# Self-attention stage of a convolution and mixture-of-experts kernel: the inverse root on ScalarE with a Newton step on VectorE, and the residual and normalising passes on GpSimd

## The chip, the cores and the metric

The kernel runs on 1 core of one Trainium2 chip. The metric is the device time of one execution in microseconds (us).

## The reference, cut to what matters

The model has a convolution-attention hybrid layer, a self-attention and a mixture of experts, on 8 images of 32 x 32 tokens with 256 channels. The change is in the self-attention, one pass per image over 1024 tokens:

```python
t = _to_tokens(x)                       # x after the hybrid layer: x + concat(conv, attention projection)
n = (t - mean(t)) / sqrt(var(t) + 1e-5)                       # _ln_t
Q, K, V = n @ W_q, n @ W_k, n @ W_v                           # 256 -> 128
w = softmax(Q @ K.T / sqrt(128))
t = t + (w @ V) @ W_o + b_o + n                               # the attention adds its own input n
# the experts then get _ln_t(t), a second normalisation of the same form
```

## The kernel before, in words

`self_attention` works image by image. 1024 tokens are 8 tiles of 128 tokens (`TT`); `QT` = 4 tiles are a half. For one image the steps are: `proj` (the earlier attention's projection: `att`, divided by the softmax sums `rsb` in the step `norm`, times `wp`, on TensorE, evicted by ScalarE into `mixT`); `mix` (transposes of `mixT`, added to `xb` by VectorE); `var` (mean and variance, `spread`, L1304); the inverse root `rstd`; `apply` (VectorE makes `shift` = -mean x rstd, ScalarE writes the normalised tokens `u`); `ut` (`u` transposed on TensorE, ScalarE rounds it to `uT_hi`, VectorE keeps the remainder `uT_lo`); `q`, `k`, `v`, `vt` (projections, each again as high and low part); `scores` (TensorE, then the row maximum on VectorE at L1312, then the exponential on ScalarE at L1227); `probs` (transposes of the probabilities, copied by ScalarE); `half` and `values` (probabilities times V); `out` (times W_o, and VectorE's b_t at L1361 adds `xb`); `vvar` and `vapply` (second normalisation, `rstdt` and `v2`, L1340); `turn` (transposes of `v2`).

The order of all engines' queues is written out by hand. An image's period has 8 slots. Each begins with `scores` of one tile, and then come the steps of `BETWEEN[slot]`, as (step, index, d): d = 0 is the image itself, d = 1 the next, d = -1 the one before. Each engine runs through the same list and does its own part, in order. Image 0 has no image before it, image 7 none after it. `FRONT` is the list for image 0's preparation ahead of the first period. `a_ps`, `b_ps` and `c_ps` are single PSUM banks: `ut` 1 can write `a_ps` only when the step `ut` 0 has been read by ScalarE and VectorE. `u` is one buffer for half an image.

What the change touches, as it is before:

- The inverse root is a power on GpSimd, 128x4 elements (L1214 for `rstd`, L1217 for `rstdt`).
- `apply` on VectorE writes `grow` = rstd + 1 and `shift` (L1327, L1328). ScalarE writes `u`, and 8 `grow` steps spread over the slots turn `xb` in place into xb x (rstd + 1) + shift, that is x + n (L1251). The step `res` adds b_o on VectorE (L1332).
- `norm`, the product `att` x `rsb`, is on VectorE (L1336), in slots 0 and 1; `proj` 0 is in slot 1 and `proj` 1 in slot 2.
- ScalarE loads its function table once, ahead of the stage (L1289): `nc.scalar.preload_act_table_set("natural_log_exp_and_others")`.
- SP loads `att` and `rsb` of the image after next once `proj` has read them.

`newton` (L46) is a helper of four dependent VectorE instructions with a drain behind each (L48, L50, L52, L54). Before, only the convolutions call it, on 128x2.

Of the kernel before, what the change touches and what calls it, by code (L numbers as in the profile page):

```python
# [7 lines left out]
ALU = mybir.AluOpType  # L8
# [962 lines left out]
def self_attention(nc, x, attn_w, attn_b, w_q, w_k, w_v, w_o, b_o, mixT_d, att_d, rsum_d, t_d, vT_d, vsum_d):  # L971
# [3 lines left out]
    with ExitStack() as ctx:  # L975
# [38 lines left out]
        vart, rstdt = (sb(f"b_{n}", [P, 2, QT]) for n in ("vart", "rstdt"))  # L1014
# [14 lines left out]
        var_ready, rstd_ready, shift_ready, u_ready, grown_ready, res_ready = (  # L1029
            sem(f"b_{n}_s") for n in ("var", "rstd", "shift", "u", "grown", "res"))  # L1030
# [38 lines left out]
        FRONT = [("norm", 0), ("norm", 1), ("proj", 0), ("proj", 1), ("mix", 0), ("mix", 1), ("mix", 2), ("var", 0), ("mix", 3), ("apply", 0), ("var", 1),  # L1069
# [28 lines left out]
        with nc.Block() as block:  # L1098
# [105 lines left out]
            @block.gpsimd  # L1204
            def _(pool):
                nc.gpsimd.memset(power[:], -0.5)
# [12 lines left out]
                all_images(pool, run)  # L1219

            @block.scalar
            def _(act):
                def run(steps):
                    for what, k, n, s in steps:
# [715 lines left out]
```

## Time and profile before

| | before |
|---|---|
| median of 3 runs | 2388.21 us |
| lowest and highest run | 2386.5 and 2390.58 us |
| the profiled execution's own time | 2386.5 us |
| its span | 2384.8 us |
| mean granted TensorE clock in it | 0.94 |
| TensorE, VectorE, ScalarE, GpSimd busy | 91%, 56%, 52%, 10% |

The profile is that of one execution, the 2386.5 us run. A row of the timeline gives start, duration (of a run of neighbouring instructions, where xcount is over 1), engine, line, operation, output <- inputs and their shapes; in brackets the idle time of the engine before it and what ended it. PE is TensorE's matmul, PEld its weight load, DVE VectorE, ACT ScalarE, POOL GpSimd, SP SyncE. The granted clock is a share of 2.4 GHz. A drain or a semaphore wait is not a row of its own.

### The profile page before, as it was taken

How to read it: one execution, taken by the hardware profiler on the slowest of the kernel's cores; microseconds unless marked ns; L12 is line 12 of the kernel's file. 1: busy time of each engine (PE TensorE's matmuls, PEld its weight loads, DVE VectorE, ACT ScalarE, POOL GpSimd, SP SyncE). 2: the span in 40 equal slices, each digit the busy share in tenths (PEclk: the TensorE clock that was granted, in tenths of full speed). 3: DMA queues.
4: the chain of work that ended last, by engine and by line, in shares of the span. 5: the costliest groups of instructions: out<-in, count | busy, mean ns of one | idle time of the engine just before them, and what ended most of it. 6: DMA issues, size and time to landing. Idle time of an engine off the chain costs nothing. (4 is left out here: it accounts for less than half of the span.)

```text
span 2384.8 us, 29739 instructions
## 1 busy us (share of the span) xinstructions
PE 2163.8 (91%) x10534; PEld 1496.6 (63%) x10534; DVE 1336.7 (56%) x1974; ACT 1234.4 (52%) x2160; POOL 249.2 (10%) x259
## 2 busy tenths in 40 slices
PE   4999999947899999999999983799999983999997
PEld 3777888846555455454554531577777772888886
DVE  6222333225777777777777712466666642565665
ACT  1111222222377777777777772466666642565664
POOL 1000000010031211222112300000000000000000
PEclk7999999965699999999999996999999996999999
DMA  2322243386776667776677303333333115334532
GB/s 74 85 83 66 67 137 119 120 165 189 214 109 118 110 106 111 109 117 109 103 118 109 111 10 93 117 102 102 105 110 107 44 54 199 124 131 177 186 123 63
DMA packets 150444, 268.01 MB, mean 112 GB/s; under 512 B 31809, under 2 KB 94017, under 8 KB 146241
## 3 DMA queue, kind: packets, MB, share of 16 engines
q1 hardware_dynamic: 141344, 240.76, 41.9%
q0 software_dynamic: 7680, 25.17, 3.3%
q8 instruction: 65, 1.06, 0.2%
q10 hardware_dynamic: 1312, 0.67, 0.1%
q14 instruction: 43, 0.34, 0.0%
HBM read 156.62 MB, written 107.25 MB: 111 GB/s over the span
## 5 line engine op out<-in xcount | busy, mean ns | idle before, releaser
L647 DVE TENSOR_REDUCE a_nmax<-a_sm 128x1 f32<-128x1024 f32 x512 | 603.8, 1219 | 195.2 <-PE a_sm L667 195.2
L903 ACT ACTIVATE p_shared<-a_st 128x512 f32<-128x512 f32 x1024 | 556.8, 597 | 234.8 <-PE a_st L928 233.2
L943 PE MATMUL a_pv<-p_shared,a_va 128*32 128x512 f32 x2048 | 272.5, 604 | 0.9 <-ACT p_shared L903 0.9
L928 PE MATMUL a_st<-a_qf,a_kf 121*128 121x512 f32 x704 | 253.8, 438 | 10.1 <-ACT p_shared L903 8.0
L667 PE MATMUL a_sm<-a_kf,a_qf 120*128 120x512 f32 x704 | 217.8, 429 | 42.3 <-DMA a_kf<-kq_d 27.5
L928 PEld LDWEIGHTS a_st<-a_qf,a_kf 121*128 121x128 f32 x704 | 119.0, 188 | 208.6 <-ACT p_shared L903 198.0
L1813 PE MATMUL x_h_ps<-x_v_hi,x_w 128*128 128x512 f32 x512 | 180.4, 394 | 25.7 <-DVE x_v_lo L1754 25.7
L667 PEld LDWEIGHTS a_sm<-a_kf,a_qf 120*128 120x128 f32 x704 | 135.9, 203 | 79.4 <-issue 27.6
L1827 PE MATMUL x_y_ps<-x_h_hi,x_w 128*128 128x512 f32 x512 | 178.0, 389 | 0.0
L1764 DVE SCALAR_TENSOR_TENSOR x_h_lo<-x_hid,x_wts,x_h_hi 128x512 fp32r<-128x512 f32 x128 | 96.0, 750 | 137.3 <-ACT x_h_hi L1735 137.3
L1731 ACT ACTIVATE x_hid<-x_h_ps,x_b 128x512 f32<-128x512 f32 x128 | 88.4, 691 | 130.2 <-PE x_h_ps L1813 125.2
L1813 PEld LDWEIGHTS x_h_ps<-x_v_hi,x_w 128*128 128x128 f32 x512 | 96.8, 189 | 45.5 <-issue 25.7
L1398 PE MATMUL b_o_ps<-b_pT,b_v 128*128 128x256 f32 x512 | 121.3, 380 | 0.0
L507 PE MATMUL c_acc<-c_y_hi,c_w_hi 128*128 128x512 f32 x288 | 117.6, 408 | 0.0
L507 PE MATMUL c_acc<-c_y_hi,c_w_hl 128*128 128x512 f32 x288 | 117.3, 407 | 0.0
L1227 ACT ACTIVATE b_probs<-b_s_ps,b_nmax 128x1024 f32<-128x1024 f32 x64 | 71.2, 1113 | 88.8 <-DVE b_nmax L1312 88.8
L507 PE MATMUL c_acc<-c_y_lo,c_w_hi 128*128 128x512 f32 x288 | 117.2, 407 | 0.0
L507 PE MATMUL c_acc<-c_y_lo,c_w_hl 128*128 128x512 f32 x288 | 117.1, 407 | 0.0
L507 PE MATMUL c_acc<-c_y_hi,c_w_lo 128*128 128x512 f32 x288 | 117.1, 406 | 0.0
L928 PE MATMUL a_st<-p_q_all,a_kf 121*128 121x512 f32 x320 | 112.4, 432 | 0.3 <-ACT p_shared L903 0.3
L1827 PEld LDWEIGHTS x_y_ps<-x_h_hi,x_w 128*128 128x128 f32 x512 | 96.1, 188 | 20.0
L928 PEld LDWEIGHTS a_st<-p_q_all,a_kf 121*128 121x128 f32 x320 | 53.7, 187 | 86.7 <-ACT p_shared L903 82.9
(242 smaller groups left out, 3609.4 us busy)
## 6 DMA issues: line engine op xcount, KB each, us to landing
x_w<-w_d SPq DMA_DIRECT2D x32, 1024.0 KB, 8.5
rel_d<-p_shared SPq DMA_DIRECT2D x12, 2048.0 KB, 12.2
a_qf<-rel_d SPq DMA_DIRECT2D x22, 512.0 KB
a_qf<-rel_d SPq DMA_DIRECT2D x44, 256.0 KB
c_xtok<-in_x SPq DMA_DIRECT2D x8, 1024.0 KB, 5.8
va_d<-c_va SPq DMA_DIRECT2D x16, 512.0 KB, 4.8
rel_d<-a_hl SPq DMA_DIRECT2D x4, 2048.0 KB, 20.7
a_va<-va_d SPq DMA_DIRECT2D x32, 256.0 KB
```

The costliest lines, as they stand in the source:

```text
L507: m = nc.tensor.matmul(image_rows(acc[u][:]), wt[:, k, :] if tap is None else wt[:, k, tap, :], y[s][:, k, rows + dy:rows + dy + H // 2, d ...
L647: nc.vector.tensor_reduce(nmax[:, h, t:t + 1], sm[k % 2][:], axis=AX.X, op=ALU.max, negate=True).then_inc(sm_read, 1)
L667: m = nc.tensor.matmul(sm[k % 2][:, cols], qf[j][0:ROW_M, h, half, t * P:(t + 1) * P], kf[j][0:ROW_M, h, cols], start=True, stop=True)
L903: nc.scalar.activation(probs[:, t % 2, h, half * HALF:(half + 1) * HALF], st[half][:], ACT.Exp).then_inc(exp_done, 1)
L928: nc.tensor.matmul(st[half][:], kf[j][0:ROW_M + 1, h, t * P:(t + 1) * P], qf[j][0:ROW_M + 1, h, 2 * t // TT, half * HALF:(half + 1) * HALF ...
L943: m = nc.tensor.matmul(pv[32 * h:32 * h + 32, cols], va[j][:, t, h, :], probs[:, t % 2, h, cols], start=t == 0, stop=t == TT - 1, skip_gro ...
L1227: nc.scalar.activation(probs[k % 2][:], s_ps[:], ACT.Exp, bias=nmax[:, k:k + 1], accum_out=ssum[:, k:k + 1]).then_inc(exp_done, 1)
L1398: m = nc.tensor.matmul(o_ps[:], v_sb[s][:, t, :], pT[k % 2][:, t, :], start=t == 0, stop=t == TT - 1)
L1731: nc.scalar.activation(hid[k % GB][:], h_ps[k % 2][:], ACT.Gelu, bias=b1_sb[s][:, e, f:f + 1]).then_inc(hid_ready, 1)
L1764: nc.vector.scalar_tensor_tensor(h_lo[k % HB][:], hid[k % GB][:], wts[s][:, e:e + 1], bits(h_hi[k % HB][:]), ALU.mult, ALU.subtract).then_ ...
L1813: m = nc.tensor.matmul(h_ps[k % 2][:], w[s][:, e, c, part, tile(f)], v[s][:, c, half(j)], start=i == 0, stop=i == 3 * KC - 1)
L1827: m = nc.tensor.matmul(y_ps[j][c][:], w[s][:, e, 2 + f // 2, part, f % 2 * C + c * P:f % 2 * C + (c + 1) * P], h[k % HB][:], start=first a ...
```

## The change

The inverse root is ScalarE's Ln and then Exp with scale -0.5, with a drain between, and VectorE then runs `newton` on the result, once in `apply` and once in `vapply`, ahead of its former work there. `grow` and `res` are gone. GpSimd instead adds `u` to `xb` and then b_o, after `u` is written; ScalarE's next `apply` waits for that, as `u` is one buffer. `norm` is done by GpSimd in its part of `proj`, and `proj` 0 moves from slot 1 to slot 0.

```diff
         BETWEEN = [
-            [("out", 2, -1), ("probs", 7, -1), ("norm", 0, 1), ("vt", 1, 0), ("turn", 0, -1), ("grow", 0, 0), ("grow", 1, 0)],
-            [("probs", 0, 0), ("proj", 0, 1), ("half", 3, -1), ("turn", 1, -1), ("norm", 1, 1), ("mix", 0, 1), ("grow", 2, 0)],
-            [("mix", 1, 1), ("values", 3, -1), ("probs", 1, 0), ("out", 3, -1), ("vvar", 1, -1), ("proj", 1, 1), ("var", 0, 1),
-             ("grow", 3, 0), ("grow", 4, 0)],
+            [("out", 2, -1), ("probs", 7, -1), ("proj", 0, 1), ("vt", 1, 0), ("turn", 0, -1)],
+            [("probs", 0, 0), ("half", 3, -1), ("turn", 1, -1), ("mix", 0, 1)],
+            [("mix", 1, 1), ("values", 3, -1), ("probs", 1, 0), ("out", 3, -1), ("vvar", 1, -1), ("proj", 1, 1), ("var", 0, 1)],
             [("probs", 2, 0), ("half", 0, 0), ("mix", 2, 1), ("apply", 0, 1), ("values", 0, 0), ("mix", 3, 1)],
             [("vapply", 1, -1), ("ut", 0, 1), ("probs", 3, 0), ("ut", 1, 1),
              ("probs", 4, 0), ("turn", 2, -1), ("var", 1, 1), ("q", 0, 1), ("v", 0, 1)],
-            [("turn", 3, -1), ("k", 0, 1), ("half", 1, 0), ("vt", 0, 1), ("apply", 1, 1), ("grow", 5, 0), ("res", 0, 0)],
-            [("out", 0, 0), ("values", 1, 0), ("ut", 2, 1), ("probs", 5, 0), ("out", 1, 0), ("ut", 3, 1), ("grow", 6, 0), ("grow", 7, 0)],
-            [("q", 1, 1), ("probs", 6, 0), ("res", 1, 0), ("vvar", 0, 0), ("half", 2, 0), ("k", 1, 1), ("vapply", 0, 0), ("v", 1, 1),
-             ("values", 2, 0)]]
+            [("turn", 3, -1), ("k", 0, 1), ("half", 1, 0), ("vt", 0, 1), ("apply", 1, 1)],
+            [("out", 0, 0), ("values", 1, 0), ("ut", 2, 1), ("probs", 5, 0), ("out", 1, 0), ("ut", 3, 1)],
+            [("q", 1, 1), ("probs", 6, 0), ("vvar", 0, 0), ("half", 2, 0), ("k", 1, 1), ("vapply", 0, 0), ("v", 1, 1), ("values", 2, 0)]]
...
             @block.gpsimd
-                        if what == "var":
-                            pool.wait_ge(var_ready, n * 2 + k + 1)
-                            nc.gpsimd.tensor_tensor(rstd[:, k], var[:, k], power[:], ALU.pow).then_inc(rstd_ready, 1)
-                        if what == "vvar":
-                            pool.wait_ge(vart_ready, n * 2 + k + 1)
-                            nc.gpsimd.tensor_tensor(rstdt[:, k], vart[:, k], power[:], ALU.pow).then_inc(rstdt_ready, 1)
+                        if what == "proj":
+                            pool.wait_ge(att_loaded[k], n * (16 * (1 + GROUPS)) + 16 * (1 + GROUPS))
+                            nc.gpsimd.tensor_tensor(att[k][:], att[k][:], rsb[k][:], ALU.mult).then_inc(norm_ready, 1)
+                        if what == "apply":
+                            x1 = xb[s][:, k * QT:(k + 1) * QT, :]
+                            pool.wait_ge(u_ready, n * 2 + k + 1)
+                            nc.gpsimd.tensor_tensor(x1, x1, u[:], ALU.add)
+                            pool.drain()
+                            pool.wait_ge(w_loaded, 16 * 5)
+                            nc.gpsimd.tensor_tensor(x1, x1, bo_all, ALU.add).then_inc(res_ready, 1)
...
             @block.scalar
+                def rsqrt(out, in_):
+                    nc.scalar.activation(out, in_, ACT.Ln)
+                    act.drain()
+                    return nc.scalar.activation(out, out, ACT.Exp, scale=-0.5)
...
+                        elif what == "var":
+                            act.wait_ge(var_ready, n * 2 + k + 1)
+                            rsqrt(rstd[:, k], var[:, k]).then_inc(rstd_ready, 1)
+                        elif what == "vvar":
+                            act.wait_ge(vart_ready, n * 2 + k + 1)
+                            rsqrt(rstdt[:, k], vart[:, k]).then_inc(rstdt_ready, 1)
                         elif what == "apply":
                             act.wait_ge(shift_ready, n * 2 + k + 1)
+                            act.wait_ge(res_ready, n * 2 + k + 1)
...
-                        elif what == "grow":
...
             @block.vector
+                def scales(m, r, v, tm, sh, ready):
+                    newton(nc, dve, r, v, tm)
+                    nc.vector.scalar_tensor_tensor(sh, m[:, :, 0], -1.0, r, ALU.mult, ALU.mult).then_inc(ready, 1)
...
                         elif what == "apply":
                             dve.wait_ge(rstd_ready, n * 2 + k + 1)
-                            nc.vector.tensor_scalar(grow[s][:, k], rstd[:, k], 1.0, None, ALU.add)
-                            nc.vector.scalar_tensor_tensor(shift[s][:, k], mv[:, :, 0], -1.0, rstd[:, k], ALU.mult, ALU.mult).then_inc(shift_ready, 1)
-                        elif what == "res":
-                            dve.wait_ge(grown_ready, n * TT + (k + 1) * QT)
-                            x1 = xb[s][:, k * QT:(k + 1) * QT, :]
-                            nc.vector.tensor_tensor(x1, x1, bo_all, ALU.add).then_inc(res_ready, 1)
-                        elif what == "norm":
-                            dve.wait_ge(att_loaded[k], n * (16 * (1 + GROUPS)) + 16 * (1 + GROUPS))
-                            nc.vector.tensor_tensor(att[k][:], att[k][:], rsb[k][:], ALU.mult).then_inc(norm_ready, 1)
+                            scales(mv, rstd[:, k], var[:, k], tmp[:, k], shift[:, k], shift_ready)
                         elif what == "vapply":
                             dve.wait_ge(rstdt_ready, n * 2 + k + 1)
+                            newton(nc, dve, rstdt[:, k], vart[:, k], tmpt[:, k])
```

## Rows read from the trace of the kernel before

**Rows 1.** Page, part 1: span, and busy time of TensorE.
```profile
span 2384.8 us, 29739 instructions
PE 2163.8 (91%) x10534; PEld 1496.6 (63%) x10534; DVE 1336.7 (56%) x1974; ACT 1234.4 (52%) x2160; POOL 249.2 (10%) x259
```

**Rows 2.** Busy time by window, one inner image (number 2).
```profile
core 0: us, PE busy (x) PEld busy (x) DVE busy (x) ACT busy (x) POOL busy (x), PEclk, DMA share, GB/s
1622.70:1680.70 58.00, 55.51 (x295) 44.43 (x294) 36.67 (x85) 37.47 (x74) 4.03 (x4) 1.00 0.33 105
```

**Rows 3.** Waits of TensorE, 1510 to 1960: total us, times, longest.
```profile
PE b_a_ps L1421 <- DVE b_uT_lo L1349: 12.0, 7, 2.5
PE b_a_ps L1421 <- ACT b_u L1245: 4.1, 6, 0.7
```

**Rows 4.** Timeline, slots 3 and 4 of image 2.
```profile
1646.27 2.07 ACT L1245 ACTIVATE b_u<-b_xb,b_shift,b_rstd 128x256 f32<-128x256 f32 x4
...
1647.84 1.22 DVE L1312 TENSOR_REDUCE b_nmax<-b_s_ps 128x1 f32<-128x1024 f32 x1 [0.70 <-PE b_s_ps L1383]
...
1648.98 1.37 DVE L1340 TENSOR_SCALAR b_v<-b_t,b_mvt,b_rstdt 128x256 f32<-128x256 f32 x4
...
1650.82 0.69 DVE L1349 TENSOR_TENSOR b_uT_lo<-b_a_ps,b_uT_hi 128x512 fp32r<-128x512 f32 x1 [0.47 <-ACT b_uT_hi L1255]
...
1651.57 0.65 PE L1421 MATMUL b_a_ps<-b_ident,b_u 128*128 128x128 f32 x4 [1.59 <-DVE b_uT_lo L1349]
```

**Rows 5.** Groups by line, GpSimd and ScalarE: busy us, mean ns, idle before.
```profile
L874 POOL TENSOR_TENSOR p_bd_lo<-a_w_st,p_bd_hi 128x512 fp32r<-128x512 f32 x32 | 41.9, 1310 | 12.9 <-issue 12.9
L266 ACT ACTIVATE c_sd<-c_gvar 128x2 f32<-128x2 f32 x8 | 1.6, 203 | 80.3 <-DVE c_gvar L324 80.3
L1289 ACT ACT_TABLE_LOAD x1 | 1.3, 1283 | 11.1 <-issue 11.1
```

**Rows 6.** Timeline of the convolutions, first image's normalisation.
```profile
26.53 5.18 POOL L244 TENSOR_TENSOR c_w_lo<-p_shared,c_w_hi 128x1152 fp32r<-128x1152 f32 x2 [20.25 <-DVE c_w_hi L435]
26.60 2.56 DVE L48 TENSOR_TENSOR c_tmp<-c_rstd 128x2 f32<-128x2 f32 x1
...
29.23 2.49 DVE L50 TENSOR_TENSOR c_tmp<-c_tmp,c_gvar 128x2 f32<-128x2 f32 x1
31.81 0.17 DVE L52 TENSOR_SCALAR c_tmp<-c_tmp 128x2 f32<-128x2 f32 x1
32.05 0.16 DVE L54 TENSOR_TENSOR c_rstd<-c_rstd,c_tmp 128x2 f32<-128x2 f32 x1
```

**Rows 7.** Timeline of the experts, one power on GpSimd.
```profile
2044.24 1.22 DVE L1754 TENSOR_TENSOR x_v_lo<-x_vT,x_v_hi 128x1024 fp32r<-128x1024 f32 x1
2044.41 1.92 POOL L1710 TENSOR_TENSOR x_rstd<-x_var,x_power 128x4 f32<-128x4 f32 x1 [55.89 <-DVE x_var L1782]
```

**Rows 8.** Tile `b_rstd`, 1480 to 1960: ns least/median/most, first and last start.
```profile
L1214 POOL TENSOR_TENSOR b_rstd<-b_var,b_power x15: 1007/1008/1013, 1481.0 to 1887.2; 128x4 f32<-128x4 f32 x15
```

**Rows 9.** Busy time by window, behind one TensorE wait in image 7.
```profile
1935.00:1939.00 4.00, 3.98 (x17) 3.66 (x18) 0.00 (x0) 1.75 (x5) 0.00 (x0) 0.57 0.00 0
```

**Rows 10.** Timeline of TensorE, three rows behind waits.
```profile
1536.54 0.66 PE L1421 MATMUL b_a_ps<-b_ident,b_u 128*128 128x128 f32 x4 [2.46 <-DVE b_uT_lo L1349]
...
1935.02 1.73 PE L1389 MATMUL b_pT_ps<-b_ident,b_probs 128*128 128x128 f32 x8 [2.68 <-ACT b_pT L1231]
...
1969.59 1.11 PE L1454 MATMUL b_c_ps<-b_ident,b_v 128*128 128x128 f32 x4 [5.67 <-DVE b_v L1340]
```

**Rows 11.** Timeline of the front, `norm` 1 of image 0.
```profile
1465.88 1.22 DVE L1336 TENSOR_TENSOR b_att<-b_att,b_rsb 128x1024 f32<-128x1024 f32 x1 [4.56 <-DMA b_rsb<-rsum_d]
```

**Rows 12.** Timeline, slot 1 of image 0.
```profile
1516.42 1.11 ACT L1227 ACTIVATE b_probs<-b_s_ps,b_nmax 128x1024 f32<-128x1024 f32 x1 [1.54 <-DVE b_nmax L1312]
...
1519.39 0.63 PE L1414 MATMUL b_a_ps<-b_ident,b_mixT 128*128 128x128 f32 x4 [1.53 <-ACT b_mixT L1238]
```

**Rows 13.** Timeline, slot 6 of image 2.
```profile
1665.18 1.10 ACT L1227 ACTIVATE b_probs<-b_s_ps,b_nmax 128x1024 f32<-128x1024 f32 x1
...
1668.10 0.60 PE L1421 MATMUL b_a_ps<-b_ident,b_u 128*128 128x128 f32 x4
```

More of the change, by code:

```diff
@@ L994, in self_attention @@
         st6, mv = sb("b_st6", [P, QT, 6]), sb("b_mv", [P, QT, 2])
-        var, rstd = (sb(f"b_{n}", [P, 2, QT]) for n in ("var", "rstd"))
-        grow, shift = ([sb(f"b_{n}{s}", [P, 2, QT]) for s in range(2)] for n in ("grow", "shift"))
-        power = sb("b_power", [P, QT])
+        var, rstd, tmp, shift = (sb(f"b_{n}", [P, 2, QT]) for n in ("var", "rstd", "tmp", "shift"))
         u = sb("b_u", [P, QT, C])
@@ L1013, in self_attention @@
         st6t, mvt = sb("b_st6t", [P, QT, 6]), sb("b_mvt", [P, QT, 2])
-        vart, rstdt = (sb(f"b_{n}", [P, 2, QT]) for n in ("vart", "rstdt"))
+        vart, rstdt, tmpt = (sb(f"b_{n}", [P, 2, QT]) for n in ("vart", "rstdt", "tmpt"))
         v2 = sb("b_v2", [P, QT, C])
@@ L1028, in self_attention @@
         c_read = sem("b_c_read")
-        var_ready, rstd_ready, shift_ready, u_ready, grown_ready, res_ready = (
-            sem(f"b_{n}_s") for n in ("var", "rstd", "shift", "u", "grown", "res"))
+        var_ready, rstd_ready, shift_ready, u_ready, res_ready = (sem(f"b_{n}_s") for n in ("var", "rstd", "shift", "u", "res"))
         uhi_ready, bhi_ready = sem("b_uhi_s"), sem("b_bhi_s")
@@ L1062, in self_attention @@
              ("probs", 4, 0), ("turn", 2, -1), ("var", 1, 1), ("q", 0, 1), ("v", 0, 1)],
-            [("turn", 3, -1), ("k", 0, 1), ("half", 1, 0), ("vt", 0, 1), ("apply", 1, 1), ("grow", 5, 0), ("res", 0, 0)],
-            [("out", 0, 0), ("values", 1, 0), ("ut", 2, 1), ("probs", 5, 0), ("out", 1, 0), ("ut", 3, 1), ("grow", 6, 0), ("grow", 7, 0)],
-            [("q", 1, 1), ("probs", 6, 0), ("res", 1, 0), ("vvar", 0, 0), ("half", 2, 0), ("k", 1, 1), ("vapply", 0, 0), ("v", 1, 1),
-             ("values", 2, 0)]]
-        FRONT = [("norm", 0), ("norm", 1), ("proj", 0), ("proj", 1), ("mix", 0), ("mix", 1), ("mix", 2), ("var", 0), ("mix", 3), ("apply", 0), ("var", 1),
+            [("turn", 3, -1), ("k", 0, 1), ("half", 1, 0), ("vt", 0, 1), ("apply", 1, 1)],
+            [("out", 0, 0), ("values", 1, 0), ("ut", 2, 1), ("probs", 5, 0), ("out", 1, 0), ("ut", 3, 1)],
+            [("q", 1, 1), ("probs", 6, 0), ("vvar", 0, 0), ("half", 2, 0), ("k", 1, 1), ("vapply", 0, 0), ("v", 1, 1), ("values", 2, 0)]]
+        FRONT = [("proj", 0), ("proj", 1), ("mix", 0), ("mix", 1), ("mix", 2), ("var", 0), ("mix", 3), ("apply", 0), ("var", 1),
                  ("ut", 0), ("ut", 1), ("apply", 1), ("sums", 0), ("q", 0), ("k", 0), ("v", 0), ("vt", 0), ("ut", 2), ("ut", 3), ("q", 1), ("k", 1), ("v", 1)]
@@ L1205, in _ @@
             def _(pool):
-                nc.gpsimd.memset(power[:], -0.5)
                 nc.gpsimd.memset(wp[:], 0.0).then_inc(consts, 1)
@@ L1211, in run @@
                     for what, k, n, s in steps:
[L1212 to L1217 removed]
+                        if what == "proj":
[8 more added lines that the diff above has]
+                            nc.gpsimd.tensor_tensor(x1, x1, bo_all, ALU.add).then_inc(res_ready, 1)
+                bo_all = bo[:].rearrange("p (a c) -> p a c", a=1).to_broadcast([P, QT, C])
                 all_images(pool, run)
@@ L1245, in run @@
                                 last = nc.scalar.activation(u[:, i, :], xb[s][:, k * QT + i, :], ACT.Identity,
-                                                            bias=shift[s][:, k, i:i + 1], scale=rstd[:, k, i:i + 1])
+                                                            bias=shift[:, k, i:i + 1], scale=rstd[:, k, i:i + 1])
                             last.then_inc(u_ready, 1)
-                        elif what == "grow":
-                            j, i = k // QT, k % QT
-                            nc.scalar.activation(xb[s][:, k, :], xb[s][:, k, :], ACT.Identity, bias=shift[s][:, j, i:i + 1],
-                                                 scale=grow[s][:, j, i:i + 1]).then_inc(grown_ready, 1)
                         elif what == "ut":
@@ L1357, in run @@
                             if k % 2 == 0:
-                                dve.wait_ge(res_ready, n * 2 + k // 2 + 1)
+                                dve.wait_ge(res_ready, n * 2 + k // 2 + 2)
                                 dve.wait_ge(t_stored[k // 2], n * 16 + 16)
@@ L1363, in run @@
                             last.then_inc(c_read, 1)
+                dve.sem_inc(res_ready, 1)
                 dve.wait_ge(sums_loaded[0], 16)
```

1 line of the change is left out of this document (removed).

## The prediction

> **What bounds the kernel now.** I read the page's busy times first [rows 1]: TensorE is busy for 91% of the span, VectorE and ScalarE for little over half, GpSimd for a tenth. The change touches one stage only, self-attention, from about 1442 to 1974 us, so I then read that stage in windows, one from each image's first scores to the next one's [rows 2]. An inner image takes 58.0 us, in which TensorE is busy for 55.5, VectorE for 36.7, ScalarE for 37.5 and GpSimd for 4.0. TensorE sets the pace, and lighter queues on VectorE and ScalarE can return only what TensorE now waits for. The waits [rows 3] say how much that is: 12.0 us for `b_uT_lo` in 7 waits and 4.1 us for `b_u` in 6. In each inner image both lie in slot 4 of `BETWEEN`. The timeline of one such place [rows 4] shows the chain: ScalarE writes `u`, VectorE takes the maximum of the scores, then does `vapply` (`b_v`), then the low part of `uT`, and TensorE, which needs its one PSUM bank back, stands until that low part is written (1.59 us). Whatever is put into VectorE's queue ahead of that low part goes straight into TensorE's wait. That is where the change must be priced.
>
> **The change part by part.** *Removed.* ScalarE loses 64 `grow` instructions, VectorE loses 16 `res` and 16 `norm` passes of 1.22 us (one of them in [rows 11]). Neither engine sets the end in the inner images, so these are worth nothing by themselves, except where named below.
>
> *GpSimd's new passes.* Per image it gets two `norm` products and four additions of 128x1024. The trace has no such pass; the nearest are 128x512 at 1.31 us [rows 5] and 128x1152 at 5.18/2 = 2.59 us [rows 6]. The slope is 1.28/640 = 2.0 ns an element, so 128x1024 is 1.31 + 512 x 0.002 = 2.33 us; bounds 1.31 and 2.59, and I take 2.33, for 1024 lies near the larger. The Trainium skill (GPSIMD Engine Reference, section "Performance versus the Vector engine") gives 4497 ns for an addition of 2048 elements, by an estimate half of it, 2.25 us, for ours; no run here shows that size, and the total would be 6 x 2 x 0.08 = 1 us lower by it. Six passes are 14 us of 58, so GpSimd's load fits easily.
>
> *Newton's step on VectorE, 32 times.* Its code also runs in the convolutions, beside long GpSimd passes, and that is the most telling place in the trace [rows 6]. The last two of its four small instructions take 0.17 and 0.16 us and start 0.24 us apart. The first two are TENSOR_TENSORs with both inputs in SBUF, on 128x2 elements, and last 2.56 and 2.49 us: the first ends at 29.16, when GpSimd's first pass ends (26.53 + 2.59 = 29.12), the second at 31.72, when its second ends. So a VectorE instruction with two SBUF inputs is held until the running two-input GpSimd pass is over. The reverse is seen among the experts [rows 7]: GpSimd's power, 1.01 us when left alone, takes 1.92 us beside a two-input VectorE pass. In the self-attention of before the same power takes 1007 to 1013 ns in all 15 cases of its window [rows 8], though much of VectorE's work with one input in PSUM runs then, so I hold only two-SBUF-input work to collide. Free of a collision a step costs 4 x 0.24 = 0.95 us.
>
> *Where they collide.* `vapply` of slot 4 now begins with Newton's step. In [rows 4] `u` of half 0 is complete at 1646.27 + 2.07 = 1648.34; GpSimd is idle and starts its first addition then, to 1650.7, and its second by about 1653.2. The step starts when the maximum ends, 1649.06, inside the first addition. Its first instruction is held to 1650.7; three more follow, and either the second or the fourth falls under the second addition and is held to about 1653.3. The step ends at 1653.5 (fourth held) to 1653.9 (second held), `vapply` takes 1.37 us more, and the low part of `uT` ends at 1653.55 + 1.4 + 0.7 = 1655.65 instead of 1651.51. TensorE's wait grows by 4.1 us, from 1.6 to 5.7. Bounds: 0.5 us (only the step, 0.95, less VectorE's slack of 0.47) and, with GpSimd passes of 2.59 us and both held, 4.9 us. It occurs where an image has both a predecessor (`vapply`) and a successor (`apply`): images 1 to 6. **6 x 4.1 = +24.6 us.**
>
> *The clock behind that wait.* After a wait of 2.68 us [rows 10] TensorE's granted clock was 0.57 on average over the next 4.0 us [rows 9], the lower level, 1.2 GHz, for most of it, and 4.0 x 0.43 = 1.7 us of work was lost; behind a wait of 5.67 us four transposes took 1.11 us, against 0.66 us behind one of 2.46 us [rows 10]. The new wait of 5.7 us is of the long kind, six times. Bounds: nothing and twice 1.7; I take 1.7, what the nearest row lost. **+10.2 us.**
>
> *Root on ScalarE instead of GpSimd.* Ln and Exp on 128x4 are bounded by nothing and 1.01 us (the power), nearest the Sqrt of 128x2 at 0.203 us [rows 5]; two and a handover are 0.47 us, less than the power. But they stand in ScalarE's queue, which waits there for the variance. Behind them stand `mixT` (slot 2), `q_hi` (slot 4) and `k_hi` (slot 7). They come about 1.7, 1.1 and 0.7 us later, against slack on TensorE of about 1.5 to 2, 0.6 beyond the delay, and 0.9. I cost this at nothing; if that slack were gone it would be up to 0.5 us in each of 7 images.
>
> *Slots 5 and 6.* Here GpSimd is idle when the step of `apply` runs, so it costs 0.95 us less 0.08 for the small addition that filled `grow`, 0.87. `u` starts that much later, but the following `grow` (0.6 us) is gone, so the exponential of 1665.18 starts 0.5 later, and so do `uT_hi`, `uT_lo` and the transposes that begin at 1668.10 [rows 13], after 0.2 us of TensorE's slack: 0.36 us in images 1 to 6 and 0.2 in image 0, **+2.4 us**.
>
> *`proj` 0 one slot earlier.* In inner images it covers a wait of 0.2 us in slot 0: **-1.2 us**. In image 0, slot 1, TensorE waited 1.53 us for `mixT` [rows 12]; with the product done a slot earlier its next scores can follow the exponential of 1516.42 by 1.26 us, at 1517.7 instead of 1519.8: **-2.1 us**. `norm` is out of the way, since GpSimd finishes the products of the next image some 2 to 3 us ahead of slot 0. SP's loads of `att` hang on `proj` and move with it; they are two slots early already.
>
> *Front and end.* `norm` 1 waits for its load until 1465.88 [rows 11] and heads the chain of the front; on GpSimd it takes 1.1 us more. The steps of `apply` 0 and 1 add 0.4 each: **+1.9 us**. At the end the last `vapply` gains 0.8 by the dropped `res` and loses about 0.5: **-0.3 us**.
>
> Sum: 24.6 + 10.2 + 2.4 - 1.2 - 2.1 + 1.9 - 0.3 = **+35.5 us**. The profiled execution took 2386.5 us, 1.7 outside its span and 1.7 below the median of the runs. 2386.5 + 35.5 = **2422 us**.
>
> **The rivals.** *A: no collision.* Newton's inputs are only 16 bytes a partition, and might slip in between. For it: the last two instructions in [rows 6] are quick; against it: the first two, of 8 bytes, were not. The terms beside it are +0.7, slot 4 costs 6 x 0.5 = 3.0: 2386.5 + 3.7 = 2390 us. *B: the relief wins (faster).* If VectorE is not held and ScalarE, rid of 38 us of `grow`, brings `u` and `uT_hi` forward, the waits of [rows 3] shrink; all 16.1 us would give 2370. It decides if the low part of `uT` in slot 4 ends before 1651.5. Against it: ScalarE starts `u` there behind a copy of probabilities, and no `grow` stands ahead of it in that slot. *C: one-SBUF-input work collides too.* Then the low parts, `t` and `mix` are held as well, about 5 us more in six images: 2452 us; [rows 8] speak against it. *D: table loads.* The stage loads its table once, by name (1.28 us, [rows 5]). If Ln and Exp each reloaded, 64 x 1.28 = 82 us would fall on ScalarE, about half on the path: 2463 us. The Trainium skill (ScalarE: Activation LUTs, section "Table sets: the hidden batching unit") has both functions in the named set, so one load, and prices a switch at about 2.7 us; were they separate, the loads would by it be 170 us and not 82. Whether Ln stays in that set no row shows, since before has none.
>
> **How the numbers follow.** Forecast 0.73, A 0.11, B 0.04, C 0.08, D 0.04. The forecast's own range: without the clock's loss and with 3.5 us a collision, 0.7 + 21 = +22 (2408); with 4.9 and twice the clock's loss, 0.7 + 29.4 + 20.4 = +50 (2437). The range reaches up over C and lets A, B and D go: 2404 to 2455. About 0.2% (4.8 us) can be told from no change. A lies near that mark, 0.08 within and 0.03 above: slower 0.73 + 0.08 + 0.04 + 0.03 = 0.88, same 0.08, faster 0.04.
>
> **What would show it.** In the timeline of slot 4, Newton's TENSOR_TENSORs lasting 1.5 to 2.5 us and ending with GpSimd's additions; TensorE's wait for `b_uT_lo` near 5.7 us six times, about 37 us in sum; the granted clock at its lower level after each; GpSimd's additions near 2.3 us; one table load in the stage. In slots 3, 5 and 7 the steps should take 0.9 us. Wrong it would be if the small instructions stay at 0.16 us beside GpSimd's passes (A), or if waits for `q_lo`, `k_lo` or `mixT` appear.

## The result, and the profile after

The changed kernel takes 2417.2 us (median of 4 runs, 2415.6 to 2418.75) and the kernel before 2387.4 us (4 runs, 2386.5 to 2390.6). The ratio is 1.0122, with a 95% interval from 1.011 to 1.0136: slower by 1.2%. The profiled execution took 2417.93 us, its span 2416.2, so 31.4 us more than the span in [rows 1]. Line numbers below are those of the kernel whose rows they are.

The head of the page of the changed kernel, against [rows 1]:

```profile
span 2416.2 us, 30025 instructions
PE 2175.0 (90%) x10534; PEld 1508.0 (62%) x10534; DVE 1342.2 (56%) x2054; ACT 1214.4 (50%) x2160; POOL 329.9 (14%) x274
```

TensorE does the same 10,534 matmuls and is busy 11.2 us longer for them, so part of the loss is slower matmuls and not idle time. VectorE is busy 5.5 us longer although 32 large passes left it.

TensorE's waits in the stage (total us, times, longest), against [rows 3]:

```profile
PE b_a_ps L1426 <- DVE b_uT_lo L1353: 35.7, 7, 5.6
PE b_a_ps L1426 <- ACT b_u L1259: 4.6, 7, 0.7
```

The wait for `b_uT_lo` has grown by 23.7 us. Its timeline in slot 4 of image 2 is the place of [rows 4]:

```profile
1652.68 1.22 DVE L1324 TENSOR_REDUCE b_nmax<-b_s_ps 128x1 f32<-128x1024 f32 x1 [0.70 <-PE b_s_ps L1388]
...
1653.27 2.35 POOL L1214 TENSOR_TENSOR b_xb<-b_xb,b_u 128x1024 f32<-128x1024 f32 x1 [30.72 <-ACT b_u L1259]
...
1653.83 1.81 DVE L48 TENSOR_TENSOR b_tmpt<-b_rstdt 128x4 f32<-128x4 f32 x1
...
1655.71 0.16 DVE L50 TENSOR_TENSOR b_tmpt<-b_tmpt,b_vart 128x4 f32<-128x4 f32 x1
1655.76 2.34 POOL L1217 TENSOR_TENSOR b_xb<-b_xb,b_bo 128x1024 f32<-128x1024 f32 x1
1655.95 2.18 DVE L52 TENSOR_SCALAR b_tmpt<-b_tmpt 128x4 f32<-128x4 f32 x1
1658.20 0.16 DVE L54 TENSOR_TENSOR b_rstdt<-b_rstdt,b_tmpt 128x4 f32<-128x4 f32 x1
1658.44 1.38 DVE L1344 TENSOR_SCALAR b_v<-b_t,b_mvt,b_rstdt 128x256 f32<-128x256 f32 x4
1659.74 0.68 DVE L1353 TENSOR_TENSOR b_uT_lo<-b_a_ps,b_uT_hi 128x512 fp32r<-128x512 f32 x1
1660.47 1.12 PE L1426 MATMUL b_a_ps<-b_ident,b_u 128*128 128x128 f32 x4 [5.64 <-DVE b_uT_lo L1353]
```

The first Newton instruction works on 128x4 elements and lasts 1.81 us; it ends at 1655.64, with GpSimd's first addition (1655.62). The second fits into the gap between the additions. The third, a TENSOR_SCALAR with one tensor read, lasts 2.18 us and ends at 1658.13, with the second addition (1658.10). What follows is late by as much, and TensorE stands for 5.64 us where it stood for 1.59. The four transposes behind it take 1.12 us instead of 0.65: the clock is down. There are six such waits of 5.64 to 5.65 us, one in each of images 1 to 6.

Images 1 and 2 from each first maximum of the scores to the next one's, by busy time (columns as in [rows 2]):

```profile
1563.93:1627.80 63.87, 57.37 (x293) 46.31 (x292) 38.25 (x95) 34.98 (x74) 14.13 (x6) 0.95 0.30 95
1627.80:1690.81 63.01, 56.52 (x295) 45.74 (x294) 38.25 (x95) 34.85 (x74) 14.14 (x6) 0.97 0.30 97
```

Measured so, the six images 1 to 6 take 379.2 us against 346.8 before, image 0 takes 51.7 against 53.95, the front from its first reciprocal to the first maximum 70.12 against 66.85, and the stages ahead of it ended 2.0 us sooner in this execution. With -0.4 for image 7 and the tail and +0.3 behind them, 32.4 - 2.25 + 3.3 - 2.0 - 0.4 + 0.3 = 31.35, the +31.4 of the spans.

### The profile page after: what moved, and what is told of

It reads as the page before. It is cut to its first block and busy times, and to the rows that moved or that the text cites. A ratio compares the mean times of both kernels' runs of the same rounds, so it can differ in the third digit from the quotient of the medians.

```text
span 2416.2 us, 30025 instructions
## 1 busy us (share of the span) xinstructions
PE 2175.0 (90%) x10534; PEld 1508.0 (62%) x10534; DVE 1342.2 (56%) x2054; ACT 1214.4 (50%) x2160; POOL 329.9 (14%) x274
## 5 line engine op out<-in xcount | busy, mean ns | idle before, releaser
L1324 DVE TENSOR_REDUCE b_nmax<-b_s_ps 128x1 f32<-128x1024 f32 x64 | 78.4, 1225 | 67.3 <-PE b_s_ps L1388 66.9
```

What stands on the lines that cost most here:

```text
L1324: nc.vector.tensor_reduce(nmax[:, k:k + 1], s_ps[:], axis=AX.X, op=ALU.max, negate=True).then_inc(max_ready, 1)
```

## The experiments

### The additions wait for `b_v`

GpSimd's additions of half 0 wait until slot 4's `vapply` is done, so that no Newton instruction of that slot meets them.

```diff
 pool.wait_ge(u_ready, n * 2 + k + 1)
+if k == 0 and not (isinstance(n, int) and n < 2):
+    pool.wait_ge(v_ready, n * 2 - 2)
```

> The changed kernel, but GpSimd starts its additions of half 0 only when the vapply of the image before has been written, so that Newton's step in slot 4 has the SBUF to itself; all engines do the same work. Theory 1 (GpSimd's passes hold VectorE's small instructions): Newton's instructions in slot 4 take 0.16 us each, TensorE's wait for b_uT_lo falls from 5.6 to about 2.1 us in six images, the clock stays high behind it, and the kernel comes to about 2388 us (-29). Rival (the cost is the longer queues on VectorE and ScalarE, not the collision): the work is the same, so 2417 us.

Measured: 2388.39 us (10 runs), ratio to the kernel before 0.9995 (0.9985 to 1.0004). One wait on GpSimd, which does the same work, gives the whole loss back. In its timeline of slot 4 Newton's instructions are short again and GpSimd starts behind `b_v`:

```profile
1648.92 0.15 DVE L48 TENSOR_TENSOR b_tmpt<-b_rstdt 128x4 f32<-128x4 f32 x1
...
1649.38 0.17 DVE L52 TENSOR_SCALAR b_tmpt<-b_tmpt 128x4 f32<-128x4 f32 x1
...
1649.87 1.38 DVE L1346 TENSOR_SCALAR b_v<-b_t,b_mvt,b_rstdt 128x256 f32<-128x256 f32 x4
...
1651.33 2.37 POOL L1216 TENSOR_TENSOR b_xb<-b_xb,b_u 128x1024 f32<-128x1024 f32 x1 [33.67 <-DVE b_v L1346]
...
1651.91 0.66 PE L1428 MATMUL b_a_ps<-b_ident,b_u 128*128 128x128 f32 x4 [1.98 <-DVE b_uT_lo L1355]
```

The wait is 1.98 us, 0.4 more than before: that is what Newton's step costs beside nothing. Images 1 to 6 take 348.0 us at a full granted clock, 5.2 us less each than in the changed kernel; 3.65 of it is the shorter wait and 1.55 is left for the clock. TensorE's busy time agrees: over the six images it is 9.9 us longer in the changed kernel for the same matmuls, 1.6 us an image.

### Newton's step out of slot 4

Is it the step itself, or the place? Two kernels take the step of slot 4 away. One moves it into slot 3:

```diff
-... ("apply", 0, 1), ("values", 0, 0), ("mix", 3, 1)],
+... ("apply", 0, 1), ("vnewton", 1, -1), ("values", 0, 0), ("mix", 3, 1)],
```

> The changed kernel, with the Newton step of vapply 1 taken out of slot 4 and put in slot 3 behind apply 0, where GpSimd is idle; same instructions, same total. Theory 1: the six waits fall to about 1.6 us and the kernel comes to about 2386 us. Rival (queue length): at most the step's own 0.95 us in six images is saved, so 2411 us or more.

The other drops it from both `vapply` steps, in slots 4 and 7:

```diff
 dve.wait_ge(rstdt_ready, n * 2 + k + 1)
-newton(nc, dve, rstdt[:, k], vart[:, k], tmpt[:, k])
 for i in range(QT):
```

> The changed kernel without Newton's step in vapply (the root of the second normalisation is left at ScalarE's Ln and Exp). What is then beside GpSimd's additions in slot 4 are the four TENSOR_SCALARs of 128x256 with their scalars from SBUF. If only instructions with two SBUF inputs are held, or this form is free: waits of 1.6 us, about 2385 us. If every TENSOR_SCALAR from SBUF to SBUF is held, as L52 was in the changed kernel (2.18 us): one or two of the four are held, the waits stay at 3.5 to 5.5 us, 2405 to 2417 us.

Measured: 2411.8 us (ratio 1.0089, 1.0072 to 1.0106) and 2412.5 us (1.0094, 1.0077 to 1.0111). Both win only 5 us, and where I had expected the first to be as fast as before, it was not. (The second lies in the range that I had given for the case that the TENSOR_SCALARs are held.) Timeline of slot 4 in the kernel without the step:

```profile
1653.23 2.36 POOL L1214 TENSOR_TENSOR b_xb<-b_xb,b_u 128x1024 f32<-128x1024 f32 x1 [30.70 <-ACT b_u L1259]
...
1653.79 5.08 DVE L1343 TENSOR_SCALAR b_v<-b_t,b_mvt,b_rstdt 128x256 f32<-128x256 f32 x4
...
1655.73 2.34 POOL L1217 TENSOR_TENSOR b_xb<-b_xb,b_bo 128x1024 f32<-128x1024 f32 x1
```

`b_v` itself, four TENSOR_SCALARs that take 1.38 us otherwise, is held over both additions, to 1658.87. The wait is 4.72 us six times in both kernels, 0.93 less than in the changed one, which is about the length of a free Newton step. So the step is the first to be caught, and not the whole cause: where it is gone, the TENSOR_SCALARs of `b_v` are caught in its place.

### One addition instead of two

GpSimd's second addition is left out.

```diff
-nc.gpsimd.tensor_tensor(x1, x1, u[:], ALU.add)
-pool.drain()
-pool.wait_ge(w_loaded, 16 * 5)
-nc.gpsimd.tensor_tensor(x1, x1, bo_all, ALU.add).then_inc(res_ready, 1)
+nc.gpsimd.tensor_tensor(x1, x1, u[:], ALU.add).then_inc(res_ready, 1)
```

> The changed kernel (2417.2 us) with GpSimd's second addition, that of b_o, left out: x1 is x + u alone (b_o is missing from the output). Theory 1 (a VectorE instruction that touches only SBUF and meets a GpSimd pass is held to the end of that pass, whatever its size): in slot 4 the first Newton instruction is held as now (about 1.8 us), the third is free at 0.17 instead of 2.18, TensorE's wait for b_uT_lo falls from 5.65 to about 3.5 us in images 1 to 6. That is 6 x 2.1 = -12.9 us, and 2 to 4 us more of the clock behind a shorter idle time: 2401 us. Theory 2 (what holds VectorE is that GpSimd is at work at all beside slot 4, so one hold grows as the other goes; or the b_v pass falls under what is left): waits stay above 5 us, 2415 to 2417 us.

Measured: 2403.3 us (ratio 1.0049, 1.0034 to 1.0064). Slot 4 of image 1, timeline:

```profile
1591.96 2.35 POOL L1214 TENSOR_TENSOR b_xb<-b_xb,b_u 128x1024 f32<-128x1024 f32 x1 [33.22 <-ACT b_u L1256]
...
1592.53 1.81 DVE L48 TENSOR_TENSOR b_tmpt<-b_rstdt 128x4 f32<-128x4 f32 x1
...
1594.65 0.17 DVE L52 TENSOR_SCALAR b_tmpt<-b_tmpt 128x4 f32<-128x4 f32 x1
...
1597.17 0.66 PE L1423 MATMUL b_a_ps<-b_ident,b_u 128*128 128x128 f32 x4 [3.64 <-DVE b_uT_lo L1350]
1597.67 1.81 PE L1391 MATMUL b_pT_ps<-b_ident,b_probs 128*128 128x128 f32 x8
```

The hold ends with the addition that is running, and the next instruction is held only if there is a next addition. The wait fell by 2.0 us, as theory 1 had it. The last row also shows that 3.64 us of standing still brought the clock down, though later: the first transposes are at full speed, the eight behind them take 1.81 us instead of 1.04. In busy time by window, images 3 and 4 of this kernel:

```profile
1688.56:1747.93 59.37, 54.77 (x292) 43.77 (x291) 36.25 (x95) 34.74 (x74) 9.41 (x4) 1.00 0.31 102
1747.93:1809.08 61.15, 56.68 (x294) 45.87 (x293) 36.25 (x94) 34.85 (x74) 9.40 (x4) 0.97 0.30 99
```

Image 3 kept the full clock and image 4 did not: 1.8 us between them. The other four are at 0.97 like image 4. The images are not quite alike, though: in the first experiment, all at the full clock, image 3 takes 57.71 us and image 4 58.27. Against the same image there, image 3 takes 1.7 us more and the other five 2.9 to 3.1, so the fallen clock costs 1.2 to 1.4 us.

### TensorE kept busy in the wait

Twelve matmuls 128x512 whose result nobody reads stand ahead of turn 1 of `u` in images 1 to 6, so that TensorE does not idle for so long and the collision stays as it is.

```diff
 elif what == "ut":
+    if k == 1 and not (isinstance(n, int) and n < 2):
+        pe.wait_ge(b_read, n * NB + b_at("q", 0) + 1)
+        for _ in range(12):
+            nc.tensor.matmul(b_ps[:], w_hi[:, 0, 0, :], w_hi[:].rearrange("p k t u -> p (k t u)")[:, 0:HALF],
+                             start=True, stop=True)
     pe.wait_ge(a_read, n * NA + a_at("ut", k) + 1)
```

> The changed kernel, with 12 matmuls without use (128x512 into a free PSUM bank, about 2.8 us) put into TensorE's wait of 5.6 us in images 1 to 6; the wait's end does not move. If the clock's fall behind the wait costs what the prediction said (1.7 us, six times): the granted clock stays at 1.00 there and the kernel comes to about 2407 us. If the slower clock is hidden: 2417 us. If 2.8 us of work are not enough to keep the clock: 2417 us with the clock still low.

Measured: 2412.3 us (ratio 1.0088, 1.0071 to 1.0104), 5 us less than the changed kernel, between the 2407 us of a clock kept everywhere and the 2417 us of one kept nowhere. Two of its images, by window:

```profile
1567.50:1629.25 61.75, 57.83 (x305) 46.18 (x304) 38.33 (x94) 34.73 (x74) 14.18 (x6) 1.00 0.30 99
...
1753.96:1817.10 63.14, 59.39 (x307) 47.94 (x306) 38.30 (x95) 34.83 (x74) 14.17 (x6) 0.97 0.29 96
```

The fill kept the clock up in four images of six. These four take 61.5 to 62.0 us, the other two 62.7 and 63.1, and those of the changed kernel 62.6 to 63.9. The four average 61.7 us against 63.2 for the six of the changed kernel, 1.5 us less. Against the same images of the first experiment the four take 3.7 to 3.8 us more and the other two 4.9 to 5.0. So a kept clock is worth 1.2 to 1.5 us an image.

### Which forms of instruction are held

A small program behind the kernel's end meets 13 forms of VectorE instruction, each once with GpSimd idle, once under an addition of two SBUF tiles and once under a multiplication of one tile by a constant.

```diff
+dve.sem_inc(go, 1)                                              # GpSimd starts its pass
+nc.vector.tensor_reduce(pad[:], acc[:], axis=AX.X, op=ALU.max)  # 0.7 us, reads PSUM
+dve.drain()
+test(form, out)
```

> The changed kernel with a small program behind its end: 13 forms of VectorE instruction, each met three times: with GpSimd idle (tile name ending in free), under a GpSimd addition of two SBUF tiles 128x1024 (ending in add), and under a GpSimd multiplication of one SBUF tile 128x1024 by a constant (ending in cpy). Each instruction starts about 0.7 us after the GpSimd pass, so that a hold to the end of the addition shows as about 1.6 us more. Theory 1 (held: what reads and writes SBUF alone, one or two inputs, except the statistics): tt_small, ts_small, stt_small, recip, ts_ptr, ts_imm, copy, tt_two about +1.6 us under the addition; tt_ps, stt_ps, copy_ps, stats, reduce within 0.1 us of free. Theory 2 (held: two SBUF inputs, and the tensor_scalar and copy forms, which run at twice the rate: 128x256 in 0.3 us rather than 0.6; everything at one element a cycle with one SBUF input is free): as theory 1 but recip and reduce, and perhaps ts_small, free; a form's free time tells which. Under the multiplication by a constant both theories leave open whether anything is held. The kernel's own part should show the times of the changed kernel; the total is longer by some 150 us.

Timeline of the first form. The test instruction ends with the addition (2424.00), and not with the multiplication (2427.00):

```profile
2421.39 0.16 DVE L1949 TENSOR_TENSOR m_tt_small_free<-m_src,m_oth 128x4 f32<-128x4 f32 x1
2421.66 2.34 POOL L1972 TENSOR_TENSOR m_o<-m_z,m_y 128x1024 f32<-128x1024 f32 x1 [0.55 <-DVEq L1991]
...
2422.45 1.57 DVE L1949 TENSOR_TENSOR m_tt_small_add<-m_src,m_oth 128x4 f32<-128x4 f32 x1
...
2424.21 2.79 POOL L1974 TENSOR_SCALAR m_o<-m_z 128x1024 f32<-128x1024 f32 x1 [0.21 <-DVEq L1987]
2424.98 0.29 DVE L1949 TENSOR_TENSOR m_tt_small_cpy<-m_src,m_oth 128x4 f32<-128x4 f32 x1
```

All 39, in ns, as the trace gives them:

| VectorE instruction | GpSimd idle | under the addition | under the multiplication |
| --- | --- | --- | --- |
| TENSOR_TENSOR, two SBUF, 128x4 | 164 | 1566 | 290 |
| SCALAR_TENSOR_TENSOR, two SBUF, 128x4 | 164 | 1583 | 285 |
| TENSOR_SCALAR, constants, 128x4 | 170 | 1597 | 283 |
| TENSOR_TENSOR, two SBUF, 128x256 | 425 | 1850 | 548 |
| TENSOR_SCALAR, scalars from SBUF, 128x256 | 414 | 1715 | 411 |
| TENSOR_SCALAR, constants, 128x256 | 295 | 1717 | 414 |
| COPY, SBUF, 128x256 | 295 | 1718 | 417 |
| RECIPROCAL, SBUF, 128x4 | 178 | 177 | 178 |
| BATCH_NORM_STATS2, SBUF, 128x256 | 428 | 427 | 428 |
| TENSOR_REDUCE, SBUF, 128x256 | 420 | 420 | 420 |
| TENSOR_TENSOR, PSUM and SBUF, 128x256 | 425 | 425 | 425 |
| SCALAR_TENSOR_TENSOR, PSUM and SBUF, 128x256 | 425 | 425 | 425 |
| COPY, PSUM, 128x256 | 424 | 424 | 425 |

Under the addition seven forms are held to its end, and six are not touched at all. Under the multiplication nothing is held, and six of those seven forms take about 0.12 us more. Theory 2 has the right list; theory 1, which had the statistics and the reduction free as well, falls with RECIPROCAL, which reads SBUF alone and is free. Theory 2's own test, that the free time tells which form is held, fails for one form: the TENSOR_SCALAR with scalars from SBUF. The Trainium skill (SBUF — State Buffer, section "Who interferes with whom") gives this list almost whole: VectorE and GpSimd share a pair of ports, which two SBUF inputs need, and which copies and TENSOR_SCALARs can take in a double-rate mode, while a reduction never does. The COPY and the TENSOR_SCALAR with constants agree (295 ns, against 424 ns for the COPY from PSUM). The one with scalars from SBUF (414 ns) shows no double rate and is held all the same. By that section whoever comes second is fully blocked; the addition agrees, the multiplication, which reads SBUF as well, does not: the measurement decides, +0.12 us and no block.

### `proj` 0 back in slot 1

From the kernel of the first experiment, one part of the change is taken back.

```diff
-[("out", 2, -1), ("probs", 7, -1), ("proj", 0, 1), ("vt", 1, 0), ("turn", 0, -1)],
-[("probs", 0, 0), ("half", 3, -1), ...
+[("out", 2, -1), ("probs", 7, -1), ("vt", 1, 0), ("turn", 0, -1)],
+[("probs", 0, 0), ("proj", 0, 1), ("half", 3, -1), ...
```

> The kernel of the first experiment (the changed kernel with GpSimd's additions behind b_v, 2388.4 us), with one part of the change taken back: projection 0 of the next image stands in slot 1 behind the first transposes again, as before the change, the division stays on GpSimd. Theory 1 (the prediction's terms of -1.2 us an inner image and -2.1 us in image 0 are right and come from this move): 2388.4 + 6 x 1.2 + 2.1 = 2397.7 us, with a wait or a stretch of lower clock ahead of slot 2 of each image. Theory 2 (the move is worth nothing, and the shorter image 0 comes from the growth's absence on ScalarE): 2388 us within 1.

What I expected here misread the prediction: its -1.2 us is the sum over the inner images, 0.2 us each, so that theory 1, by the prediction's own terms, is 2388.4 + 1.2 + 2.1 = 2391.7 us.

Measured: 2392.8 us, ratio 1.0009 (1.0 to 1.0018), against 0.9995 of the kernel that it differs from: the move is worth some 3 to 4.5 us, close to the 3.3 us of the prediction. In its trace image 0 takes 53.77 us against 51.71, and the wait of [rows 12] is back. Images 1 to 5 take 0.4 us more on average. Image 6 takes 1.5 us more, because TensorE's granted clock fell in it (0.97 over the image, 0.83 from 1892 to 1900 us) behind the same wait of 2.0 us for `b_uT_lo` that left the clock full in the other five images.

```profile
1523.50 0.63 PE L1421 MATMUL b_a_ps<-b_ident,b_mixT 128*128 128x128 f32 x4 [1.53 <-ACT b_mixT L1247]
```

### Image 0's divisions on VectorE

```diff
-if what == "proj":
+if what == "proj" and not (isinstance(n, int) and n == 0):     # GpSimd
...
+elif what == "proj" and isinstance(n, int) and n == 0:          # VectorE
+    dve.wait_ge(att_loaded[k], 16 * (1 + GROUPS))
+    nc.vector.tensor_tensor(att[k][:], att[k][:], rsb[k][:], ALU.mult).then_inc(norm_ready, 1)
```

> The kernel of the first experiment (2388.4 us) with the two divisions of image 0, in the front, on VectorE rather than on GpSimd. Theory 1 (the front's +3.2 us against the kernel before are the longer GpSimd passes ahead of projections 0 and 1, 2.34 us each against 1.2 to 1.3 on VectorE): front shorter by 2 to 3.2 us, 2385.7 us. Theory 2 (the front is longer for the additions of u on GpSimd, or for transfers): 2388 us, front as in the first experiment.

Measured: 2389.9 us, ratio 0.9994 (0.9985 to 1.0003), against 0.9995 of the kernel it starts from. In the profiled execution the front is 4.0 us shorter (66.2 us against 70.2). Most of that is TensorE's clock: projection 1 ran at the full clock (1.90 us instead of 3.67), and the transposes of `mixT` behind it are through in 5.4 us instead of 6.8. Projection 1 itself starts 0.7 us sooner. The ratios show nothing of it, and each is known to about 2 us either way. What the divisions cost in the front is left open between nothing and some 3 us.

### Towards a faster order

Three kernels try to get rid of the 2 us that are left. The first starts from the kernel of the last experiment and takes the first low part ahead of `b_v`:

```diff
-[("vapply", 1, -1), ("ut", 0, 1), ("probs", 3, 0), ("ut", 1, 1),
+[("ut", 0, 1), ("vapply", 1, -1), ("probs", 3, 0), ("ut", 1, 1),
```

> The kernel of the experiment with image 0's divisions on VectorE (GpSimd's additions behind b_v; 2389.9 us, ratio 0.9994), with one step moved: in slot 4 VectorE subtracts the low part of turn 0 of b_u before it writes b_v rather than behind it (GpSimd's additions wait for b_v as before and start 0.7 us later). In the profile of the first experiment ScalarE's high part was ready at 1650.73 and VectorE's low part began at 1651.17. Theory 1 (VectorE's b_v is what is late): the wait of 2.0 us falls by 0.45, 7 x 0.45 = -3 us, 2386.5 us. Theory 2 (ScalarE's high part, behind the exponential, is what is late, and b_v then delays the second low part, which began 1651.17 + 2.06): what is won ahead of the second turn is lost behind it, 2389 to 2391 us.

The second also puts scores 5 into the gap; the third does that to the kernel before:

```diff
+[("ut", 0, 1), ("vapply", 1, -1), ("probs", 3, 0)],
+[("ut", 1, 1), ("probs", 4, 0), ("turn", 2, -1), ("half", 1, 0), ("var", 1, 1), ("q", 0, 1), ("v", 0, 1),
+ ("turn", 3, -1), ("k", 0, 1), ("vt", 0, 1), ("apply", 1, 1)],
```

> As the previous kernel, and slot 4 is cut short: scores 5 now stand behind the transposes of probabilities 3 and ahead of turn 1 of b_u, where TensorE waited 2.0 us (5.65 in the changed kernel), and the values' first half follows turn (2). So 1.47 us of matmuls fill the gap. Theory 1 (the wait for b_uT_lo costs its own length, as the six waits did): wait 0.5 us rather than 2.0, 7 x 1.5 = -10 us, and 1 to 3 us of the clock: 2377 to 2379 us. Theory 2 (the gap moves: VectorE's maximum of scores 5 and ScalarE's exponential now stand ahead of the second low part, so the products of q and v wait instead): 2386 to 2395 us, with a wait for b_uT_lo ahead of b_q.

> The kernel before (2389.3 us), with only the order of slots 4 and 5 of the previous kernel (first low part ahead of b_v, scores 5 ahead of turn 1, the values' first half ahead of the products of q). It tells whether what that order wins or loses hangs on the change. Theory 1 (the order alone does it): the same step as the previous kernel takes, 2377 to 2379 us where that one gains. Theory 2 (VectorE's passes of the kernel before, 1.22 us for x + b_o and for each division, are then in the way): 3 us or more above the previous kernel.

Measured: 2395.5 us (ratio 1.0027, 1.0016 to 1.0038), 2397.7 us (1.0036, 1.0022 to 1.005) and 2385.0 us (0.9986, 0.9977 to 0.9995). The first is 6 to 8 us slower (by medians and by ratios; 10 us in images 1 to 6 of the two traces) than the kernel it starts from, which neither theory had. Its timeline, slot 4 of image 2:

```profile
1656.34 2.40 POOL L1216 TENSOR_TENSOR b_xb<-b_xb,b_u 128x1024 f32<-128x1024 f32 x1 [36.12 <-DVE b_v L1346]
...
1658.43 0.38 DVE L1313 BATCH_NORM_AGGREGATE b_mv<-b_st 128x2 f32<-128x6 f32 x4
1658.87 2.40 POOL L1219 TENSOR_TENSOR b_xb<-b_xb,b_bo 128x1024 f32<-128x1024 f32 x1
1658.88 2.42 DVE L1315 TENSOR_SCALAR b_var<-b_mv 128x4 f32<-128x4 f32 x1
...
1661.33 0.20 ACT L1228 ACTIVATE b_rstd<-b_var 128x4 f32<-128x4 f32 x1 [3.41 <-DVE b_var L1315]
```

Against the maximum of scores 4 the additions start 2.5 us later than in the first experiment, and now it is the one small TENSOR_SCALAR at the end of the statistics that falls under the second of them, for its whole length: 2.42 us. (In the first experiment the same instruction met the addition's last 0.3 us, and took 0.32 us.) ScalarE waits for it with `b_q_hi` behind its root. The statistics themselves, beside the first addition, were not slowed. The hold is there in images 1 to 5, and these take 59.8 to 60.3 us, each 1.9 to 2.1 more than in the kernel that this one starts from. In image 6 the second addition starts at 1899.04 and the small instruction at 1899.05, as close as in the rows above, but there it takes 0.17 us, the addition 2.44, and the image only 0.4 us more. Which of the two got in first would explain it; starts 0.01 us apart can't show that.

In the second kernel no group of VectorE's instructions is lengthened, but TensorE waits 21 us in images 1 to 6 against 12 us in the third. The waits that the second has in addition are for `b_v` (3.8 us) and `b_q_lo` (2.8 us), behind which stand Newton's step and ScalarE's root; that these two are the cause was not tried. Its new wait for `b_uT_lo`, ahead of the product of q, is theory 2's, whose range ended 3 us lower. The third is 0.14% faster than the kernel before, the only one here whose interval lies below 1, and it holds nothing of the change. So the same order gains 3 to 4 us without the change and loses about 8 us with it, which neither theory for the third kernel had.

## Why the prediction was right, and where its steps were off

The forecast was 2422 us and slower; 2417.2 was measured. The place, the six waits and the clock behind them were right; the rule of which instruction is held was wrong, and that its size came out is in part luck. Step by step:

- **GpSimd's passes.** 2.33 us forecast; their means are 2.36 us (x + u and b_o) and 2.38 us (the division).
- **The collision.** It is where it was said to be, six times, and is the main cause: taking it away alone, with the clock's fall behind it, gives 2388.4 us. Forecast 4.1 us each and a wait of 5.7 us; measured 4.05 and 5.65, six times 4.05 = 24.3 us (forecast 24.6).
- **Its rule failed.** "I hold only two-SBUF-input work to collide", drawn from [rows 6], is too narrow. The second hold fell on the third instruction, a TENSOR_SCALAR with one tensor input, which the prediction had thought immune, and not on the second or fourth. In [rows 6] that same instruction took 0.17 us only because GpSimd's passes were over at 31.7. The size came out right because whichever of the three is caught ends with the same second addition: for this number the wrong rule cost nothing. The section of the Trainium skill named at the table above lists TENSOR_SCALAR among the forms that can collide, and would have pointed to the third instruction. The narrow rule would have gone wrong for `b_v`: the kernel without Newton's step was the test, and by that rule it would have been nearly as fast as before.
- **The clock.** Forecast 1.7 us an image, +10.2. By the first experiment 1.55 us an image are left beside the shorter wait; by the filled waits it is 1.2 to 1.5. Six times 1.55 is about 9 us.
- **Root on ScalarE.** Ln and Exp take 0.206 and 0.205 us, and no wait for `q_lo`, `k_lo` or `mixT` grew: nothing, as costed.
- **Slots 5 and 6, `proj` 0.** Image 0 won 2.25 us for 2.1. By the experiment on `proj` 0 the move is worth 0.4 us an inner image where the clock stays up, 2.3 us in all, where the forecast had 0.2 and 1.2: mis-sized by about 1 us. Slots 5 and 6 were too high by as much: in the first experiment images 1 to 6 take 1.2 us more than before, of which 6 x 0.4 = 2.4 is the longer wait and about -2.3 `proj` 0, so +1.1 is left against 2.4. No run takes this step by itself, so the 1.1 is what is left over and not a measured cost.
- **Front.** +3.3 us in the traces, +1.9 forecast. Projection 1 starts 1.65 us later (forecast 1.1). `u` comes another 1.6 later, and the forecast had 0.4 for the step of `apply` 0: 1.3 of the 1.6 is again the clock, a term that the prediction did not have here. Behind projection 1 the granted clock averages 0.80 before and 0.50 in the changed kernel, and the four groups of transposes of `mixT` take 1.12 us each, where three of the four took 0.66 to 0.77. The runs can't confirm the sum (the experiment on image 0's divisions).
- **Rivals.** A (no collision) is refuted by 1.81 and 2.18 us on 128x4. B needed the relief of ScalarE to count; free of the collision the change gives 2388 us, as before, so no such gain is seen. C was half right on forms and wrong on places: TENSOR_SCALAR and COPY with one input are held when they go from SBUF to SBUF, but `b_uT_lo`, `b_t` and `mix`, which read PSUM, are not. D: the stage has one table load, of 1.28 us.

The parts of +31.4 us against the forecast's +35.5, from the two traces: collision 24.3 for 24.6, clock about 9 for 10.2, the rest of images 1 to 6 about -1 for +1.2, image 0 -2.25 for -2.1, front +3.3 for +1.9, tail -0.4 for -0.3, and -1.7 outside what the change touches. The small terms were off by up to 2.3 us either way and in part cancel.

## What to carry to other kernels

Before work goes to GpSimd, list what VectorE does from SBUF to SBUF in the same stretch, small instructions first (all but RECIPROCAL, the statistics and reductions, by the table above): each that meets a two-input GpSimd pass costs up to that pass's whole length, and everything queued behind it pays as well. A wait that lets GpSimd start behind them can be worth more than the offload (about 29 us here), but the passes then land on the next such instruction, so look where they end. An idle time of TensorE is to be priced with the clock behind it: here 1.2 to 1.5 us for each wait of 3.6 to 5.6 us behind which it fell.

## What the runs showed of the hardware

- An addition on GpSimd with two SBUF inputs holds VectorE's TENSOR_TENSOR, SCALAR_TENSOR_TENSOR, TENSOR_SCALAR and COPY from SBUF to SBUF until it ends, at 16 bytes a partition (0.16 to 1.57 us) as at 1024. RECIPROCAL, the statistics, a reduction from SBUF, and the three forms that read PSUM pass beside it in their free time, to within 1 ns. Each form was met once by itself; the kernels show the holds of TENSOR_TENSOR and TENSOR_SCALAR again in every inner image. Why the TENSOR_SCALAR with scalars from SBUF is among them, at 414 ns, is left open.
- A multiplication by a constant on GpSimd (one SBUF input, 2.77 us) holds nothing; both theories had left that open. Six of the seven forms that the addition holds take about 0.12 us more under it, at 128x4 (164 to 290 ns) as at 128x256 (295 to 417 ns); the TENSOR_SCALAR with scalars from SBUF takes none (414 and 411 ns).
- GpSimd's additions hardly pay themselves: 2.34 us in the small program, 2.40 at most in the rows above.
- A VectorE instruction that starts within about 0.05 us of the addition can pass free: Newton's second (0.16 us, started 0.05 us ahead of the second addition), and the small TENSOR_SCALAR of image 6 in the first kernel with the new order (0.17 us, recorded 0.01 us behind it), where the same instruction was held for 2.40 to 2.42 us in images 1 to 5.
- TensorE's clock stayed up behind waits of 1.98 us in all inner images of the first experiment, and in five of six of the kernel with `proj` 0 back in slot 1; it fell in five of six behind 3.64 us, and in all six behind 5.64 us. So the length of the wait alone does not settle it.
